# GpSimd's row transfers numbered, each issued once the one two before it has landed

## The reference

```
tokens = patches @ W.T + b; prepend class token; times pos_embed    # 2352 -> 128
h = tokens + lstm(layernorm(tokens))      # 65 steps in sequence, 128 images side by side
xt = layernorm(h)
probs = softmax(xt @ router_w.T + router_b); top 2 of 16 experts per token
out = h + sum over the 2 experts of gate * (gelu(xt @ w1.T + b1) @ w2.T + b2)   # 128 -> 512 -> 128
```

## Time and profile before

| | |
|---|---|
| median of three runs | 675.6 us |
| profiled execution, first to last instruction (its span) | 771.4 us |
| PE busy | 647.2 us, 84% |
| DVE busy | 562.3 us, 73% |
| POOL busy | 413.1 us, 54% |
| POOL, 130 row transfers (L1235) | 149.2 us, mean 1148 ns |
| POOL, 160 scatters of results (L1257) | 157.0 us, mean 981 ns |

### The profile page before, as it was taken

One profiled execution on the slowest core, in us unless ns is written; L12 is line 12 of the kernel. 1 busy time (PEld: TensorE's weight loads), 2 busy tenths in 40 slices (PEclk: granted clock), 3 DMA queues, 4 the chain that ended last, 5 costly groups with the idle time before them and its releaser, 6 DMA issues.

```text
span 771.4 us, 24553 instructions
## 1 busy us (share of the span) xinstructions
PE 647.2 (84%) x7952; PEld 594.7 (77%) x7952; DVE 562.3 (73%) x1797; ACT 493.0 (64%) x1259; POOL 413.1 (54%) x446
## 2 busy tenths in 40 slices
PE   4999999999999999988877665878888787888870
PEld 4999999999999999888875554766666666666660
DVE  3877888888888888778886444756565756677777
ACT  4678876766667666554446343657666767777783
POOL 0243344777767666655656646545555555545552
PEclk9999999999999999999997767999999999999995
DMA  8987877888888887765522222344323234444555
GB/s 318 372 263 271 277 253 251 261 267 256 276 261 267 276 244 236 236 213 182 162 64 60 71 63 73 108 123 119 111 78 98 78 93 118 138 137 131 170 177 195
DMA packets 71895, 141.67 MB, mean 184 GB/s; under 512 B 13078, under 2 KB 55650, under 8 KB 63838
## 3 DMA queue, kind: packets, MB, share of 16 engines
q1 hardware_dynamic: 62128, 121.69, 50.1%
q0 software_dynamic: 9280, 17.21, 6.4%
q10 hardware_dynamic: 366, 1.21, 0.5%
HBM read 116.35 MB, written 25.66 MB: 184 GB/s over the span
## 4 chain that ended last, share of the span: by engine, by line
PE 25%; DVE 24%; another core or an unknown queue 13%; issue 13%; ACT 4%; POOL 3%; DMA 1%; POOLq 0%; ACTq 0%; DVEq 0%; SPq 0%
PE pair L1279 14%; DVE patches L1099 7%; PE pair L1434 3%; DVE patches L1121 2%; PE pair L1325 2%; POOL sent L1235 2%; ACT pair L680 2%; PE pair L1452 2%; PE pair L1289 1%; DVE patches L1114 1%; DVE h L1172 1%; DVE patches L1107 1%; DVE patches L1132 1%; DVE field L843 1%
## 5 line engine op out<-in xcount | busy, mean ns | idle before, releaser
L1257 POOL DMA_INDIRECT back<-patches x160 | 157.0, 981 | 150.6 <-DVE patches L1114 104.6
L680 ACT ACTIVATE pair<-pair,b1s 128x256 f32<-128x256 f32 x320 | 126.3, 448 | 110.4 <-remote 51.5
L1279 PE MATMUL pair<-field,patches 128*128 128x128 f32 (+1 forms) x1408 | 173.9, 280 | 8.9 <-DMA patches<-in_x 8.6
L1279 PEld LDWEIGHTS pair<-field,patches 128*128 128x128 f32 (+1 forms) x1408 | 164.6, 194 | 9.6 <-issue 8.6
L1235 POOL DMA_INDIRECT sent<-pay,slot_own x130 | 149.2, 1148 | 40.3 <-issue 38.2
L1434 PE MATMUL pair<-patches,ex_hi 128*128 128x256 f16 x640 | 119.4, 280 | 47.8 <-DVE patches L1099 23.8
L605 ACT ACTIVATE gate<-pair,lbias 128x128 f32<-128x128 f32 x260 | 74.4, 369 | 98.1 <-PE pair L1294 88.6
L1452 PE MATMUL pair<-ex_hi,patches 128*128 x1280 | 117.4, 225 | 8.3 <-issue 6.1
L1247 POOL TENSOR_TENSOR rstd<-veps,cst 128x2 f32<-128x2 f32 (+1 forms) x68 | 58.0, 853 | 107.2 <-DVE veps L800 106.6
L1107 DVE CAST patches<-pair 128x256 f16<-128x256 f32 x80 | 33.7, 422 | 109.6 <-remote 105.2
L1434 PEld LDWEIGHTS pair<-patches,ex_hi 128*128 x640 | 56.6, 99 | 72.8 <-issue 64.0
(11 more groups left out here) (150 smaller groups left out, 1257.7 us busy)
## 6 DMA issues: line engine op xcount, KB each, us to landing
patches<-in_x SPq DMA_DIRECT2D x62, 1152.0 KB
patches<-sent SPq DMA_DIRECT2D x80, 130.0 KB
field<-in_we SPq DMA_DIRECT2D x64, 128.0 KB
field<-back SPq DMA_DIRECT2D x10, 768.0 KB
patches<-in_b SPq DMA_DIRECT2D x80, 64.0 KB
field<-in_pos SPq DMA_DIRECT2D x65, 64.0 KB
out_tower<-h SPq DMA_DIRECT2D x10, 384.0 KB
back<-patches POOLq DMA_INDIRECT x160
```

Of the source, the lines that this page charges most:

```text
L680: last = act.activation(up[:, cols], up[:, cols], ACT.Gelu, bias=b1s[:, bass.ds(e * FC + 2 * half + i, 1)], scale=1.0 / E_SCALE)
L1257: pool.indirect_dma_start(back, bass.IndirectOffsetOnAxis(ap=dsti[j % NO][:, k:k + 1], axis=0), yo[j % NO][:, k, :], None, bounds_check=2 ...
L1279: last = pe.matmul(bank_of, l, w_, start=(c == KS and k == 0), stop=(c == KS - 1 and k == 2))
```

## The change

Row transfers get numbers in the order in which POOL issues them (`issue_order`, `ISSUED`). The 24 semaphores `sent_done` are replaced by eight, `landed`; transfer k raises number k mod 8. Before POOL issues transfer k it waits until transfer k-2 has landed (`IN_FLIGHT = 2`). `rows_sent` becomes a wait for the second transfer of position t and the one numbered before it; the callers that waited for 8 or 24 positions now wait for the last of them. The scatters of results at L1257 keep their issue conditions.

```diff
--- before.py
+++ after.py
@@ -74,6 +74,8 @@
 assert (2 * P * FIRST_SPAN - E) // ROWS + E <= FIRST_IN
 
 NO = 12
+LANDINGS = 8
+IN_FLIGHT = 2
 
 
 C_ID, C_TRI, C_ONE, C_IOTA, C_EBASE, C_TOK, C_BSC, C_POW, C_J = np.cumsum([0, P, P, P, UG * E, E, T, 4, 1]).tolist()
@@ -290,7 +292,7 @@
         logit_ps = sem("logit_ps")
         r_logits, r_dve, r_rank = sem("r_logits"), sem("r_dve"), sem("r_rank")
         ids_done = sem("ids_done")
-        sent_done = [sem(f"sent_done{i}") for i in range(NP)]
+        landed = [sem(f"landed{i}") for i in range(LANDINGS)]
         ex_in = [sem(f"ex_in{i}") for i in range(NE)]
         ex_hi_done, ex_lo_done = sem("ex_hi_done"), sem("ex_lo_done")
         tabs_clear = sem("tabs_clear")
@@ -393,6 +395,24 @@
                     room -= 1
             return slots
 
+        def issue_order():
+
+            sends, order = send_slots(), []
+            for n in range(-5, AHEAD + TILES_B + 4):
+                order += [("row", t, choice) for t, choice in sends.get(n, ())]
+            return {what: k for k, what in enumerate(order)}
+
+        ISSUED = issue_order()
+
+        def landing(eng, k):
+
+            eng.wait_ge(landed[k % LANDINGS], 16 * (k // LANDINGS + 1))
+
+        def landed_to(eng, k):
+
+            for i in range(max(k - IN_FLIGHT + 1, 0), k + 1):
+                landing(eng, i)
+
         PLAN_A, PLAN_B = ready(EARLY_GROUPS - 1), ready(GROUPS - 1)
         assert PLAN_A + 7 <= AHEAD - 3 and PLAN_B + 8 <= AHEAD + EARLY - 3
 
@@ -431,7 +451,8 @@
             return region[bass.ds(row, ROWS), :].rearrange("(p a) w -> p a w", a=HALVES)
 
         def rows_sent(eng, t):
-            eng.wait_ge(sent_done[t % NP], (t // NP + 1) * 32)
+
+            landed_to(eng, ISSUED["row", t, 1])
 
         def patches_in(eng, t):
             eng.wait_ge(x_in[(t - 1) % NX], ((t - 1) // NX + 1) * 32)
@@ -517,11 +538,9 @@
                     if j == 0:
                         sp.wait_ge(tok_done, (T - 1 - 3))
                         sp.wait_ge(lo_done, (T - 1 - 3))
-                        for t in range(STARTS[EARLY_GROUPS] - NP, STARTS[EARLY_GROUPS]):
-                            rows_sent(sp, t)
+                        rows_sent(sp, STARTS[EARLY_GROUPS] - 1)
                     if j == EARLY:
-                        for t in range(T - NP, T):
-                            rows_sent(sp, t)
+                        rows_sent(sp, T - 1)
                         sp.wait_ge(pads, 16 * (E + 1))
                     tiles_planned(sp, j)
                     if j >= 4:
@@ -1215,13 +1234,11 @@
                     if routed(g) + 1 == n:
                         pool.wait_ge(r_dve, (g + 1) * R)
                         if g >= 4:
-                            for k in range(STARTS[g - 4], STARTS[g - 3]):
-                                rows_sent(pool, k)
+                            rows_sent(pool, STARTS[g - 3] - 1)
                         m, a = SIZES[g], STARTS[g] % NP
                         pool.tensor_copy(slot_own[:, g % 4, :, 0:m], slotf[:, :, 0:m]).then_inc(ids_done, 1)
-                        for k in range(STARTS[g], STARTS[g + 1]):
-                            if k >= NP:
-                                rows_sent(pool, k - NP)
+                        if STARTS[g + 1] > NP:
+                            rows_sent(pool, STARTS[g + 1] - 1 - NP)
                         pool.tensor_copy(pay[:, a:a + m, HID:ROW], tag[:, STARTS[g]:STARTS[g + 1], :]
                                          ).then_inc(tagged, 1)
                 for i, (t, choice) in enumerate(sends.get(n, ())):
@@ -1232,10 +1249,13 @@
                         pool.wait_ge(ids_done, (g + 1))
                         through(pool, tagged, g)
                         through(pool, yn_done, t)
+                    k = ISSUED["row", t, choice]
+                    if k >= IN_FLIGHT:
+                        landing(pool, k - IN_FLIGHT)
                     pool.indirect_dma_start(
                         sent, bass.IndirectOffsetOnAxis(ap=slot_own[:, g % 4, choice, col:col + 1], axis=0),
                         pay[:, t % NP, :], None, bounds_check=E * CAP - 1, oob_is_err=False
-                    ).then_inc(sent_done[t % NP], 16)
+                    ).then_inc(landed[k % LANDINGS], 16)
                 if both and n > AHEAD and len(sends.get(n, ())) < 2:
                     power(n, both)
```

## The result

The change makes the kernel slower: 726.24 us median (724.47 to 741.09) against 676.64, a ratio of 1.074 (95% interval 1.070 to 1.077). The forecast was 676.5 with a range of 673 to 687. One run of the changed kernel (741.09) and one of e5_hold_two (706.24) fell in a slower state of the chip; they count in the medians and are left out of the ratios.

The account below looks back on a forecast made before the run. PE was taken to set the loop's step, with POOL's power due in every step. Waits cost 0.8 us, more and fewer waits nothing, queued scatters nothing: 675.6 + 0.8, rounded, 676.5 us, range 673 to 687.

Parts of the forecast that it names:

- When a row transfer lands: Row transfers: second lands about 5.25 us after POOL is done with it, plus 0.4 us until a waiting engine sees it.
- The prediction's first step: Loop step at 146 us: next second transfer held 1.8 us to 155.46, power 0.22 us late, inside the cover.
- the cover of 0.4: Loop steps of two: POOL's power may come 0.4 us late, by gaps on DVE and before PE, without cost.
- The same replay: POOL's program over 130 row transfers, variances at old times: 28 held, 34.7 us, excess 0.8 us.
- Holds that feed themselves: Rival, loop: landings keep their distance from issue, second transfers recur after 6.6 us; 15.4 us over cover, 691 us; chance 0.16.
- No relief: Rival, POOL: held transfers meet other DVE work and take 1.89 us again; 6.3 us, 682 us; chance 0.14.
- part 1: Waits of row transfers on POOL: held ones start after DVE's long subtraction, take 0.97 us; cost 0.8 us in all.
- No transfer is held: Rival, row transfers: in unprofiled runs landings come early enough that the change does nothing; 675.6 us; chance 0.12.
- less crowding: Rival, DMA engines: fewer row transfers let loads and signals through sooner, at most 3.5 us; 672 us; chance 0.10.
- part 3: Scatters of results behind row transfers on POOL after 406 us: four holds of 0.2 to 0.95 us fit gaps, costing nothing.

Follow-up runs that it names:

- e5_hold_two: The changed kernel with only the first 60 transfers (steps of two) waiting for k-2, later ones for k-8, timed against the kernel before: 693.08 us, ratio 1.026.
- e11_own_wait: The changed kernel with transfers waiting for k-8, each step's first also for POOL's own power just before it, against the kernel before: 675.66 us, ratio 1.0031.
- e10_thin_after: The changed kernel with the patches' loads cut to a ninth from position 5 on, timed against the kernel before: 691.18 us, ratio 1.025.
- e12_hold_rest: The changed kernel with only transfers from 104 on waiting for k-2, the others for k-8, timed against the kernel before: 683.03 us, ratio 1.013.
- e2_flight8: The changed kernel with transfer k waiting for k-8 instead of k-2, numbering and eight semaphores kept, against the kernel before: 674.53 us, ratio 1.0005.
- e1_before_again: The kernel before, unchanged, run again for a second profile: 675.99 us, span 674.2 us.

## Why the prediction was wrong

**Wrong: what a hold costs.** The step that failed is in "When a row transfer lands": "A landing reaches a waiting engine somewhat later ... I take 0.4 us." The rows for it showed when SP's waiting instruction ended, not when a transfer on POOL starts. The 0.4 us for the signal was about right: in the trace of before, the last recorded landing signal for the second transfer of the step shown is at 155.58, where the prediction has 155.46. What it put at nothing is the time from the signal to the start. After the change, nearly all of the held transfers start 0.79 to 0.89 us after the landing signal of k-2; e11_own_wait measured 0.81 to 0.98 by itself. A transfer that need not wait starts 0.19 or 0.30 us after the instruction before it; why waiting costs more is not shown. From the last packet of k-2 to the start lie 1.27 us in the commonest case. The prediction's first step shows what follows: with 1.27 the second transfer starts at 156.33 instead of 155.46, and the power 1.1 us late instead of 0.22, far over the cover of 0.4.

**Wrong by counting: landings.** Packets were cut into groups of 32 in order of time. Where two transfers are in the queue at once, stragglers of the earlier one fall into the next group. After the change a good part of the held transfers start 2.0 to 2.8 us after "their" landing counted in this way, but 0.79 to 0.89 us after its signal in the trace. So these landings were taken too early. By the signals, second transfers in steps of two of the second profile of before land 6.66 us after their start (median); by the packets it was 5.77.

**Mis-sized: holds and sum.** Forecast 28 holds, 34.7 us, 0.8 us over the cover; the profile shows 52 and 123.1 us, and 42.6 us in the loop. The same replay with 1.27 us gives, as a rough estimate, 35 to 40 holds, some 50 us, and about 10 us over the cover. Some 8 us more are the fallen clock, which has no term in the prediction (estimate above). The rest I put down to feedback that a replay at old times can't have: a late power delays PE, with it everything timed by PE, the next patches' load included, and that load delays the next landing. This is argued, not shown.

**The rivals.** *Holds that feed themselves* named what happened, but with too small a price (15.4 us) and too few steps (13; second transfers were held in 24 of the 30 steps of two). After the change second transfers in steps of two land 5.63 us after their start, against 6.66 in the second profile of before: the landing moved partly with the issue. With 0.79 us to the next start this makes 6.42 us from one second transfer to the next, near the rival's 6.6 and the mean step measured, (311.29 - 149.44) / 25 = 6.47 us between transposes of `xn`. That the holds in steps of two need the load is shown by e10_thin_after; how much of the loop's 42.6 us is the start and how much the moved landings, no run separates. The prediction held against this rival; they show an indirect transfer behind one load, not what happens when it is issued later. *No relief* did not occur: the held transfer at 175.14 takes 0.97 us on POOL, and the median of all fell from 1035 to 984 ns, as part 1 said. *No transfer is held* is refuted by 123.1 us of waits, *less crowding* by the depths of 4 and 3, which are no faster than 8. The unprofiled runs were 12% shorter than the first profile's span (675.6 against 771.4), not 14; no term rests on it.

**Wrong: part 3.** "Four holds of 0.2 to 0.95 us go there into gaps": e12_hold_rest holds nine times, 17.7 us, and loses about 9 us. At the closest spacing there, 1.28 us, k-2 starts 2.56 us before k would, while the landing signal comes 2.29 us after the start at the earliest and the next start 0.79 us after that. The scatters behind them all move.

**Right.** Before the change PE sets the step in steps of two, and the margin is the path variances, power, `xn`. Held transfers pass DVE's long subtraction. Semaphores and numbering are free (e2_flight8). The surplus of the first profile's span lay outside the loop's first half (e1_before_again), so the rows on steps of two could be used as they stood.

## What to carry to other kernels

Before an engine that also has work on the critical path is made to wait for its own transfers, add up the whole round trip as that engine sees it, transfer's start to landing, signal, and start of the next, and compare it with the spacing of the transfers: here 5.6 us to the landing signal and 0.8 us to the next start, with two in flight, exceed a step of 5.72, while three in flight cost 0.6%. A transfer that had to wait started 0.8 to 1.0 us after its release, so a wait must be priced at the waiting instruction's start, not at the semaphore. And a queue limited to few in flight is a stream with a rate: taking it off the critical path in one place (the power) moved much of the loss to what stands behind its end, 33.6 of 50 us. Look at the granted clock as well: PE, made to wait, ran part of its next work at 1.2 GHz, 7.7 us of the 42.6 by the estimate.

## What the runs showed of the hardware that was not expected

An indirect transfer on POOL that waits for a semaphore starts 0.8 to 1.0 us after its release (the changed kernel, e11_own_wait); one that does not wait starts 0.19 to 0.30 us after the instruction before it. The indirect queue got no packet through in 3.6 us in which the patches' loads moved 0.92 MB, and with the change, cutting these loads to a ninth brought the landing of second transfers in steps of two from 5.63 to 3.52 us after the start (e10_thin_after). Around waits of PE for `xn` of 2.3 to 5.3 us the granted clock fell to 0.50 (1.2 GHz) four times between 130 us and the end of the changed kernel's loop, and not once there in the second profile of before.
